# Cross-attention on one core: the last tile's output in eight PSUM banks, its first pieces among the scores' and U's last steps

## The reference

```python
q   = heads(x @ W_q)
p_t = softmax(q @ heads(text @ W_k).T * scale)
txt = p_t @ heads(text @ W_v)
sem = l2norm(p_t @ text) @ l2norm(ip).T
p_i = softmax(q @ heads(ip @ W_k_ip).T * scale + 0.5 * sem) * mask
out = (txt + p_i @ heads(ip @ W_v_ip)) @ W_out + b_out + x
```

## Time and profile before

| | us |
|---|---|
| median of 3 runs | 1032.5 (1031.4 to 1037.69) |
| the profiled execution, its own time | 1031.25 |
| its span in the trace | 1029.5 |
| TensorE busy | 975.6 (95% of the span) |
| VectorE / ScalarE / GpSimd busy | 795.9 / 705.6 / 640.5 |
| mean granted TensorE clock | 0.988 |

### The profile page before, as it was taken

The page is one execution under the profiler, slowest core; times in us unless marked ns, Lnnn a source line. Parts: engine busy times, 40 slices in busy tenths (PEclk is TensorE's granted clock), DMA queues, the critical chain, the costliest instruction groups (busy, mean ns, idle before and its releaser), DMA issues.

```text
span 1029.5 us, 24562 instructions
## 1 busy us (share of the span) xinstructions
PE 975.6 (95%) x7604; PEld 795.8 (77%) x7604; DVE 795.9 (77%) x2401; ACT 705.6 (69%) x2315; POOL 640.5 (62%) x1899
## 2 busy tenths in 40 slices
PE   7986788999999999999999999999999999999877
PEld 5755566888878888888878888888878888888755
DVE  4375678888878787888878888878888888887861
ACT  1355678777677777768767777777777777787720
POOL 1112467777676667667666767766766677676750
PEclk9999989999999999999999999999999999999989
DMA  9845989879799998888899999888989979778852
GB/s 301 316 139 138 193 152 169 172 167 186 159 190 177 188 190 174 164 176 172 158 189 194 189 167 184 160 177 168 178 179 202 180 169 186 138 160 147 159 109 89
DMA packets 483871, 180.26 MB, mean 175 GB/s; under 512 B 449517, under 2 KB 461855, under 8 KB 483740
## 3 DMA queue, kind: packets, MB, share of 16 engines
q1 hardware_dynamic: 483708, 178.62, 84.2%
q10 hardware_dynamic: 32, 0.07, 0.0%
HBM read 42.34 MB, written 27.22 MB: 68 GB/s over the span
## 4 chain that ended last, share of the span: by engine, by line
PE 77%; DMA 4%; DVE 3%; SPq 3%; ACT 2%; issue 2%; POOL 1%; POOLq 0%; DVEq 0%; ACTq 0%
PE ps_O L1164 26%; PE ps_Q L1198 25%; PE ps_S L1122 12%; PE ps_U L1184 11%; DMA pts<-ph 3%; PE ps_M L1138 3%; ACT pr L905 1%; SPq L825 1%; SPq L795 1%; DMA x_in<-in_x_dram 1%; SPq L785 0%; DVE pr L1060 0%; DVE n L1072 0%; POOL ph L987 0%; DVE w_sem L1055 0%
## 5 line engine op out<-in xcount | busy, mean ns | idle before, releaser
L987 POOL TENSOR_TENSOR ph<-pr,ph 128x220 f16<-128x220 f32 (+1 forms) x640 | 273.8, 459 | 136.5 <-ACT ph L917 136.2
L905 ACT ACTIVATE pr<-ps_S,bias 128x73 f32<-128x73 f32 x1280 | 290.1, 339 | 89.0 <-DVE bias L1021 87.0
L1164 PE MATMUL ps_O<-wo_hi,aT 128*128 128x320 f16 x1280 | 295.1, 302 | 5.6 <-DVE x_in L1006 3.5
L1198 PE MATMUL ps_Q<-xT,wq_hi 128*128 128x512 f32 x800 | 280.6, 416 | 5.9 <-DVE qT L994 5.7
L917 ACT ACTIVATE ph<-pr 128x292 f16<-128x292 f32 x640 | 234.2, 440 | 5.5 <-DMA pts<-ph 0.4
L1164 PE MATMUL ps_O<-wo_lo,aT 128*128 128x320 f16 x640 | 192.7, 301 | 0.0
L1184 PE MATMUL ps_U<-xm,pts 128*128 128x110 f16 (+1 forms) x2560 | 159.5, 213 | 17.9 <-DMA pts<-ph 15.4
L1198 PEld LDWEIGHTS ps_Q<-xT,wq_hi 128*128 128x128 f32 x800 | 146.5, 191 | 33.6 <-DVE qT L994 7.0
L1184 PEld LDWEIGHTS ps_U<-xm,pts 128*128 128x128 f16 (+1 forms) x2560 | 145.1, 98 | 34.9 <-issue 12.4
L1164 PEld LDWEIGHTS ps_O<-wo_hi,aT 128*128 128x128 f16 x1280 | 125.7, 98 | 57.4 <-DVE x_in L1006 4.0
L1122 PEld LDWEIGHTS ps_S<-kbd,qT 128*128 128x128 f32 x960 | 149.9, 189 | 23.2 <-issue 9.2
(11 more groups left out here) (185 smaller groups left out, 1235.3 us busy)
## 6 DMA issues: line engine op xcount, KB each, us to landing
out_dram<-x_in SPq DMA_DIRECT2D x64, 320.0 KB, 2.6
x_in<-in_x_dram SPq DMA_DIRECT2D x56, 320.0 KB, 3.2
pts<-ph SPq DMA_TRANSPOSE x320, 3.3
aT<-in_L_xattn_W_k_dram SPq DMA_DIRECT2D x5, 512.0 KB, 8.7
w_ip<-in_L_xattn_W_k_ip_dram SPq DMA_DIRECT2D x1, 2560.0 KB, 11.6
w_v<-in_L_xattn_W_v_dram SPq DMA_DIRECT2D x1, 2560.0 KB, 18.9
w_ip<-in_L_xattn_W_v_ip_dram SPq DMA_DIRECT2D x1, 2560.0 KB, 9.3
x_in<-in_x_dram SPq DMA_DIRECT2D x2, 1280.0 KB, 12.2
```

Source lines behind the costliest of these rows:

```text
L905: last = nc.scalar.activation(pr[p % P_RING][:, j, h, :], sc[:, j, h, 0:T], ACT.Exp, bias=bias[p % 2][:, j, h:h + 1], scale=SCALE)
L987: nc.gpsimd.tensor_tensor(lo, full[:, :, t0:t1], one[:, :, 0, t0:t1], ALU.subtract).then_inc(pl_ready, 1)
L1164: last = nc.tensor.matmul(o_bank[half % 2][:, 0:HALF], stationary, moving, start=(k, a, b_) == O_MMS[0], stop=(k, a, b_) == O_MMS[-1])
L1198: last = nc.tensor.matmul(ps_Q[:], wq[a][:, c, k * P:(k + 1) * P], xT[(CC * i + c) % XT_RING][b_][:], start=(c, a, b_) == Q_MMS[0], stop=( ...
```

## The change

The output of tiles 0 to 14 stays as it is (`out_at` now ends at tile 14). Tile 15 gets its own schedule, `END_AT`, in steps 160 to 166, with one PSUM bank for each half: those of q, of x's transposes, the two of the scores, the two of U, and the two of the output. Its 17 matmuls a half are cut in parts of 6 (slots 0, 1 of `aT`), 6 (slots 2, 3), 3 (slot 4) and 2 (`ipT`). Parts 0 and 1 of halves 0 to 5 are put behind tile 14's pieces of the same step, and in steps 160 and 161 in front of U of pairs 158 and 159. In step 166 come parts 0 and 1 of halves 6 and 7, then part 2 of all halves, then part 3 of all halves. The DVE adds all eight halves in step 167. SyncE issues tile 14's stores at the end of their step, behind the transposes, and tile 15's four stores after the loop.

```diff
+    END_PARTS = (O_MMS[:6], O_MMS[6:12], O_MMS[12:15], O_MMS[15:])
+    end_bank = [ps_Q, ps_M, *g["ps_S"], *g["ps_U"], *o_bank]
-    FIRST, LAST = -4, STEPS * (TILES + 1) + 8
+    FIRST, LAST = -4, PAIRS + 8
+    END_AT = {0: ((0, 0), (1, 0)), 1: ((2, 0), (3, 0)), 2: ((0, 1), (1, 1)), 3: ((2, 1), (3, 1)),
+              4: ((4, 0), (4, 1)), 5: ((5, 0), (5, 1)),
+              6: ((6, 0), (6, 1), (7, 0), (7, 1), *((half, part) for part in (2, 3) for half in range(OUTS)))}
+    ENDS = PAIRS + max(END_AT)
@@ out_at
-        ... if 0 <= i - 1 < TILES else []
+        ... if 0 <= i - 1 < TILES - 1 else []
@@ sync: store_outputs(p) holds what stood here, for tiles 0 to 14
+                if p < PAIRS:
+                    store_outputs(p)
...
+                if p >= PAIRS:
+                    store_outputs(p)
+            for q in range(SUB):
+                store_output(TILES - 1, q)
@@ vector, at the head of the step
+                if p == ENDS + 1:
+                    for half in range(OUTS):
+                        v.wait_ge(o_ready, OUTS * (TILES - 1) + half + 1)
+                        dst = x_in[(TILES - 1) % X_RING][:, half // 2, (half % 2) * HALF:(half % 2 + 1) * HALF]
+                        nc.vector.scalar_tensor_tensor(out=dst, in0=end_bank[half][:, 0:HALF], scalar=inv_out, in1=dst,
+                                                       op0=ALU.mult, op1=ALU.add).then_inc(o_added, 1)
@@ tensor, between the pieces of out_at(p) and U; output_matmuls(i, half, mms, bank) is the old inner loop
+                for half, part in END_AT.get(p - PAIRS, ()):
+                    i = TILES - 1
+                    if part == 0:
+                        if half == 0:
+                            pe.wait_ge(q_lo, ALL_SLOTS)
+                        elif half == 1:
+                            pe.wait_ge(xT_lo, CC * TILES)
+                        elif half == 2:
+                            pe.wait_ge(s_read, PAIRS)
+                            pe.wait_ge(p_ready, PAIRS)
+                        elif half == 4:
+                            pe.wait_ge(attn_ready, PAIRS)
+                        elif half >= 6:
+                            pe.wait_ge(o_added, OUTS * i - OUTS + half + 1)
+                    if half == 0:
+                        for k in ((0, 1), (2, 3), (4,), ())[part]:
+                            pe.wait_ge(*ring(aT_loaded, CC * i + k))
+                        if part == 3:
+                            pe.wait_ge(*ring(ipT_loaded, i))
+                    last = output_matmuls(i, half, END_PARTS[part], end_bank[half])
+                    if part == 3:
+                        last.then_inc(o_ready, 1)
```

More of the change, by code:

```diff
@@ L747, in out_at @@
         i, at = divmod(p - OUT_FROM, STEPS)
-        return [(i - 1, half, piece) for half, piece in OUT_AT[at + OUT_FROM]] if 0 <= i - 1 < TILES else []
+        return [(i - 1, half, piece) for half, piece in OUT_AT[at + OUT_FROM]] if 0 <= i - 1 < TILES - 1 else []
     def ip_at(p):
@@ L773, in store_values, with store_output, store_outputs @@
                                  xb[pair][t0:t1, :, part]).then_inc(x_d_stored[pair], 16)
+            def store_output(i, q):
+                sp.wait_ge(o_added, OUTS * i + 2 * q + 2)
+                sp.dma_start(rows(out, i)[:, q], x_in[i % X_RING][:, q, :]).then_inc(x_stored[i % X_RING], 16)
+            def store_outputs(p):
+                for i in range(TILES - 1):
+                    if p - STEPS * (i + 1) in STORE_AT:
+                        store_output(i, STORE_AT[p - STEPS * (i + 1)])
             for p in range(FIRST, LAST):
@@ L1106, in _, with output_matmuls @@
         def _(pe):
+            def output_matmuls(i, half, mms, bank):
+                q, h = divmod(half, 2)
+                cols = slice(h * HALF, (h + 1) * HALF)
+                for k, a, b_ in mms:
+                    if k < CC:
+                        stationary, moving = aT[(CC * i + k) % AT_RING][:, a * SUB + q, :], wo[b_][:, k, cols]
+                    else:
+                        rows_used = slice(0, IP_STACK[a])
+                        stationary = ipT[i % IT_RING][rows_used, 2 * q + a, :]
+                        moving = vw[i // NI % VW_RING][rows_used, b_, cols]
+                    last = nc.tensor.matmul(bank[:, 0:HALF], stationary, moving,
+                                            start=(k, a, b_) == O_MMS[0], stop=(k, a, b_) == O_MMS[-1])
+                return last
             m_free = None
@@ L1142, in _ @@
                 for i, half, piece in out_at(p):
-                    q, h = divmod(half, 2)
                     n = OUTS * i + half
@@ L1155, in _ @@
                             pe.wait_ge(vw_loaded[b % VW_RING], 64 * (b // VW_RING + 1) + 16)
[L1156 to L1165, removed]
-                    if piece == len(O_PIECES) - 1:
+                    last = output_matmuls(i, half, O_PIECES[piece], o_bank[half % 2])
+                    if piece == len(O_PIECES) - 1:
+                        last.then_inc(o_ready, 1)
[20 more added lines that the diff above has]
+                    if part == 3:
                         last.then_inc(o_ready, 1)
```

## The result

The changed kernel takes 1027.53 us (median of 9 runs, 1024.97 to 1029.56); the kernel before, on the same chips, 1033.86 (9 runs, 1027.84 to 1037.69). The ratio is 0.9941, with a 95% interval of 0.9922 to 0.9960: 4 to 8 us less. The forecast was 1027.5 us, within the 1% that counts as no change. The number is met, but its base was not: the median of before was 1032.5 when the forecast was made, so the forecast difference was 4.3 to 5 us, and the measured one of the medians is 6.3.

A forecast was written before the change was run, and what follows sets the result against it. TensorE's work was taken to bound the end. Its schedule, one clock fall, eight adds and the last store gave a span of 1025.2 instead of 1029.5; 1027.0 from the profiled execution, 1028.2 from the median, so 1027.5, range 1024.5 to 1031.0.

The forecast's parts named there:

- TensorE's work bounds the end: From 996.6 TensorE has 163 output matmuls at 0.136 us, 22.2 us, and no reason to stop.
- The new wait and its length: Step 162, ahead of parts 1 of halves 0 and 1: TensorE idle 2.4 us for `aT` of slot 78.
- U late by 0.5 and 1.0 us, at no cost: U of pairs 158 and 159 start later behind tile 15's early matmuls; this costs the end nothing.
- The wide end, 1.0: Upper bound, in us, on the delay that late U of pair 159 passes to the chain of `f`, `y`, `pip`.
- The tail: After TensorE's last matmuls: eight adds at 0.46 us instead of one add, 1.1 us more than before.
- the check by the gaps: Cross-check: 7.5 us idle and 1.7 low clock go; 2.4, 1.7 and 1.1 of tail come; -4.0 us.
- The stores: Reordered tile 14 stores cost nothing; tile 15's four closely spaced stores don't disturb each other, the last taking 2.7 us.
- the slower rival: Tile 15's stores pile up at 69 GB/s: span +9.3 us, 1040.6 to 1041.8; chance 0.03.
- I count one, 1.7 us as above: TensorE's clock falls once to its lower level behind the new 2.4 us gap, costing 1.7 us; 0 as other end.
- No fall of the clock: Rival: all the same without the 1.7 us, span -5.9 us, 1025.4 to 1026.6; chance 0.37.
- my likeliest case: The clock falls behind the new gap, as summed: -4.3 us; chance 0.45.

The follow-up runs named there:

- e6_order: Changed kernel with tile 14's half 5 ahead of the parts needing `aT` of slot 78; from step 160's first output matmul to span end (local time) 39.2 us.
- e7_early: Changed kernel with the DVE's add of tile 14's half 3 at the head of step 161 instead of 162; local time 38.8 us.
- e8_behind_u: Changed kernel with parts 0 of halves 0 to 3 in step 162, behind both U, instead of 160 and 161; local time 38.9 us, ratio to before 0.9924.
- e2_both: Changed kernel with both the edits of e6_order and e7_early; local time 36.6 us, ratio to before 0.9911.
- e3_best: Changed kernel with the edits of e2_both and e5_merge together; local time 35.4 us, ratio to before 0.9891.
- e5_merge: Changed kernel with parts 2 and 3 of each half together, nothing else; local time 39.3 us, ratio to before 0.9930.
- e9_stores: Changed kernel with tile 14's stores back in their old place in SyncE's queue, ahead of the step's transposes; local time 40.6 us.
- e1_again: The changed kernel once more, without edit, for a second profile; local time 39.05 us, ratio to before 0.9942.
- e4_late: Changed kernel with eight banks and the `ipT` split, but nothing of tile 15 ahead of step 166; local time 44.2 us, ratio to before 0.9982.

## Why the prediction was right, and where not

- **TensorE's work bounds the end: right.** 163 matmuls at 0.136 us, 22.2 us from the end of the gap. In the change they would be through at 1000.90 + 22.17 = 1023.07. The last four start from 1022.53 on, so the last one at 1022.94, which is 22.04 us or 162 pitches of 0.136 behind 1000.90: no idle time in between. Part 3 begins at 1020.88 and the first add at 1021.35, 0.47 us later (0.46 was worked out).
- **The new wait and its length: right.** Forecast 2.4 us, released by `aT` of slot 78; measured 2.26 to 2.45. That half 5 stood behind it at no cost is shown by e6_order and e7_early.
- **U late by 0.5 and 1.0 us, at no cost: right** (0.53 and 0.99). The chain was delayed by none of the 0.1 to 0.3 us that I took. The wide end, 1.0, is excluded by e8_behind_u.
- **The tail: right, with a slip in its price.** Seven pitches of 0.46 and one add of 0.55 from 1021.35 end at 1025.1, and 2.7 us later the span ends:

```profile
1022.53 0.71 PE L1143 MATMUL ps_O<-vw,ipT 128*128 128x320 f16 x4
...
1024.11 1.00 DVE L1031 SCALAR_TENSOR_TENSOR x_in<-ps_O,inv,x_in 128x320 f32<-128x320 f32 x2
```

  The forecast called this 1.1 us more than before. Its own figures give 1.3: from the start of the last matmul to the end of the last add were 0.33 + 0.55 = 0.88 us, and with seven more adds, each 0.19 us longer (0.46 - 0.27) than TensorE takes to finish the next half, it is 2.2. The change's rows show 1025.11 - 1022.94 = 2.17, and e2_both against e3_best puts the price at 1.2. The forecast time doesn't hang on this, since its schedule goes through the eight adds one by one; only the check by the gaps does, and comes to -3.8 instead of -4.0.
- **The stores: right.** Neither their new place nor their closeness cost anything. The last one still took 2.7 us from its add to the end of the span. While the stores went out, the DMA engines moved 335 GB/s in a microsecond, far over the 135 below which the slower rival decides:

```profile
1024.00:1025.00 1.00, 0.00 (x0) 0.00 (x0) 1.00 (x3) 0.00 (x0) 0.00 (x0) 1.00 0.85 335
```

- **The step that failed: "I count one, 1.7 us as above".** The size of the term was right: 1.6 us in e5_merge and e9_stores. That it comes was wrong for the profile of the change, and for most others: behind this gap the clock fell in e5_merge (2.45 us) and e9_stores (2.39), and not in the change (2.27), e1_again (2.44), e7_early (2.26) and e6_order (2.59). That is two of six, so the term, weighed by how often it came, was some 0.6 us (2/6 of 1.7), and the difference -5.3 us. Without a fall the forecast was -5.9 and the local time says -6.15 and -5.9 (e1_again); the rival "No fall of the clock", to which I gave 0.37, describes the profile better than my likeliest case. The gaps in a few rows of one profile looked like a threshold between 2.04 and 2.10 us. Gaps of the same length in the same code went either way, so the length alone is none; what decides stays open.
- **Why the time was met all the same.** I placed 1027.5 between a sum from the profiled execution (1027.0) and one from the median (1028.2). The median of before turned out 1.4 us higher and the gain about as much larger, and the two cancelled. So that the time was met to 0.1 us is luck; that the gain was 4 to 8 us is not.

The interval of the ratio, 4 to 8 us, holds the difference with and without a fall. It is the profiles, not the times, that decide between them.

## What to carry to other kernels

Where a chain ends in one long row of work behind a late arrival, ask first how much of that work fits into the engine's earlier gaps, and then how much of it truly needs the arrival: here the first question was worth some 5 us, 1.6 of them by way of the clock, and the second, with the tail that came with it, less than 1 (e4_late). A gap can have two releasers close together (here 0.15 to 0.3 us apart), and then each fix alone measures as nothing and the pair as all of it. When programs differ only near their end, compare from an anchor just ahead of the edit: it gave answers to 0.2 us where whole runs scatter by 5 and more. The anchor isn't quite neutral: with the full clock behind the new gap, the local time was 38.8 to 38.9 where the clock had fallen a few microseconds ahead of the anchor (the change, e7_early, e8_behind_u), and 39.05 and 39.2 where it hadn't (e1_again, e6_order).

## What the runs showed that I had not expected

- The clock's fall is not decided by the length of the gap alone. Beside the six above there are the gaps ahead of the scores of pair 159, where TensorE waited in nearly the same way each time. Twelve profiles have this gap, and the clock fell behind it in six: after 2.44 to 2.65 us, while in the other six it stayed up after 2.49 to 2.65. For example, with 2.49 us in e8_behind_u the granted clock then fell to 0.50 (1.2 GHz), with 2.54 us in e1_again it stayed at 1.00 (2.4 GHz). In e8_behind_u, two microseconds behind the gap, which ended at 979.69:

```profile
981.00:982.00 1.00, 1.00 (x6) 0.53 (x4) 0.89 (x3) 0.11 (x2) 1.00 (x4) 0.50 0.06 17
```

  In e1_again, where it ended at 980.99:

```profile
982.00:983.00 1.00, 1.00 (x9) 0.71 (x9) 0.89 (x3) 0.34 (x2) 1.00 (x3) 1.00 0.30 57
983.00:984.00 1.00, 1.00 (x10) 0.72 (x8) 0.21 (x1) 0.75 (x4) 1.00 (x3) 1.00 0.05 11
```

- Two executions of unchanged code can reach the main loop more than 3 us apart (85.43 and 88.69), as much as half of what this change brings.
